# A graph layer on one Trainium2 core: the low one-hots of two degree counts compare with the fp32 row of lane numbers instead of the bf16 row

## Reference

```python
ones = jnp.ones_like(src, dtype=jnp.int32)
in_deg  = jnp.minimum(jax.ops.segment_sum(ones, dst, num_segments=6250), 511)
out_deg = jnp.minimum(jax.ops.segment_sum(ones, src, num_segments=6250), 511)
...
return x + z_in[in_deg] + z_out[out_deg] + cent_term + vor_term + sum3d
```

## Time and profile before

| | |
|---|---|
| median of 3 runs | 2517.13 us (2512.78 to 2529.91) |
| the profiled execution, its time | 2511.43 us |
| its span | 2509.7 us |
| mean granted PE clock | 0.835 |
| busy: PE, DVE, ACT, POOL | 1656.7, 1395.1, 739.9, 1349.8 us |
| DMA | 414.34 MB, mean 165 GB/s |

### The profile page before, as it was taken

How to read it: one execution, slowest core, us unless ns; L and a number is a source line. 1 busy time by engine, 2 the same in 40 slices (tenths; PEclk the granted TensorE clock), 3 DMA queues, 4 the chain that set the end, 5 groups by cost and what they waited for, 6 DMA issues and landing times.

```text
span 2509.7 us, 37689 instructions
## 1 busy us (share of the span) xinstructions
PE 1656.7 (66%) x11883; PEld 1320.7 (53%) x11883; DVE 1395.1 (56%) x3342; ACT 739.9 (29%) x1615; POOL 1349.8 (54%) x1290
## 2 busy tenths in 40 slices
PE   4313424554455334515699998777957999999997
PEld 0001313332223212303588887677845898888886
DVE  5345213432345323413688876877995666666664
ACT  0000112221222111301054443067743443344342
POOL 5474757767677667667200018820004676667664
PEclk9955657776677667757799999999967999999999
DMA  8232434444445444433244559987154998999995
GB/s 267 74 89 67 118 106 128 145 127 132 141 133 151 126 134 124 118 110 89 67 123 133 131 144 240 265 229 199 66 185 140 275 269 266 275 263 268 269 266 150
DMA packets 380659, 414.34 MB, mean 165 GB/s; under 512 B 50006, under 2 KB 295438, under 8 KB 380462
## 3 DMA queue, kind: packets, MB, share of 16 engines
q1 hardware_dynamic: 220120, 218.17, 28.8%
q0 software_dynamic: 57952, 92.15, 14.6%
q10 hardware_dynamic: 102390, 101.63, 13.9%
HBM read 316.11 MB, written 95.67 MB: 164 GB/s over the span
## 4 chain that ended last, share of the span: by engine, by line
PE 30%; DVE 13%; issue 7%; another core or an unknown queue 2%; ACTq 2%; ACT 1%; DVEq 1%; DMA 1%; SPq 0%; POOL 0%; POOLq 0%
PE bank L926 11%; PE bank L940 11%; DVE big L1188 3%; PE bank L699 3%; DVE big L1201 2%; DVE hotB L1233 1%; ACTq L2053 1%; PE bank L912 1%; DVE hotA L1231 1%; PE bank L679 1%; DVEq L1188 1%; PE bank L840 1%; DVE stats L1452 1%; DVE big L1209 1%
## 5 line engine op out<-in xcount | busy, mean ns | idle before, releaser
L1893 POOL DMA_INDIRECT sorted_rows<-edge_rows,sorted_pos x780 | 800.4, 1026 | 387.0 <-issue 221.8
L806 PE MATMUL bank<-mixw,xnT 128*128 128x512 f32 x392 | 234.7, 754 | 303.1 <-ACT mixw L1747 160.8
L1845 ACT ACTIVATE mixw<-bank,edge_rows 128x256 f32<-128x256 f32 (+1 forms) x456 | 238.5, 549 | 341.6 <-PE bank L926 191.4
L806 PEld LDWEIGHTS bank<-mixw,xnT 128*128 128x128 f32 x392 | 92.3, 248 | 417.1 <-issue 416.6
L926 PE MATMUL bank<-edge_rows,big 128*128 128x256 f16 (+1 forms) x2736 | 293.0, 266 | 11.1 <-issue 8.6
L940 PE MATMUL bank<-big 128*128 128x256 f16 x2520 | 284.4, 273 | 1.0 <-issue 1.0
L926 PEld LDWEIGHTS bank<-edge_rows,big 128*128 128x128 f16 x2736 | 250.1, 98 | 45.7 <-issue 10.4
L1956 POOL DMA_INDIRECT state<-xn_rows,edge_rows x105 | 116.5, 1110 | 274.8 <-DVE edge_rows L1584 243.1
L940 PEld LDWEIGHTS bank<-big 128*128 128x128 f16 x2520 | 244.2, 98 | 28.5 <-issue 1.3
L1978 POOL DMA_INDIRECT result<-mixw,edge_rows x105 | 173.2, 1650 | 139.5 <-DVE mixw L1626 76.2
L1188 DVE TENSOR_TENSOR big<-big,bank 128x128 f32 x592 | 169.5, 286 | 94.7 <-remote 14.0
(11 more groups left out here) (362 smaller groups left out, 2860.5 us busy)
## 6 DMA issues: line engine op xcount, KB each, us to landing
big<-w_parts SPq DMA_DIRECT2D x114, 1024.0 KB
edge_rows<-edge_attr SPq DMA_DIRECT2D x78, 640.0 KB
big<-sorted_rows ACTq DMA_DIRECT2D x296, 129.0 KB
big<-sorted_rows SPq DMA_DIRECT2D x128, 129.0 KB
big<-L_ffn_W ACTq DMA_DIRECT2D x128, 128.0 KB
w_parts<-big ACTq DMA_DIRECT2D x64, 256.0 KB
mixw<-sorted_rows ACTq DMA_DIRECT2D x104, 129.0 KB
sorted_rows<-edge_rows,sorted_pos POOLq DMA_INDIRECT x780
```

Of the source, the lines that this page charges most:

```text
L806: ins = e.matmul(ps_kv[h], xnT[:, t % 2, k, :], kvw[:, k, h * INNER:(h + 1) * INNER], start=(k == 0), stop=(k == KC - 1))
L1845: e.activation(h32[:, h, w], ps_h[h % 4][:, w], ACT.Gelu, bias=m_r[:, n, h:h + 1], scale=m_r[:, n, HC:HC + 1]).then_inc(gelu_done, 1)
L1893: e.indirect_dma_start(sorted_rows, bass.IndirectOffsetOnAxis(ap=row_pos[:, c:c + 1], axis=0), rows, None, bounds_check=last_row, oob_is_e ...
```

## The change

The helper gets a parameter for the row of lane numbers, and the two places that make low one-hots for the degree counts pass `iota` (fp32) in place of `iotab` (bf16). The number of instructions, their order, their waits, the other operand and the output (bf16) stay. The high one-hots (L1067, L1231) keep `iotab`.

```diff
-    def one_hots(out, n, width, values, c0):
+    def one_hots(out, n, width, values, c0, numbers=iotab):
...
-                iotab[:, 0:width].rearrange("p (b r) -> p b r", r=2).unsqueeze(1).to_broadcast([P, n, half, 2]),
+                numbers[:, 0:width].rearrange("p (b r) -> p b r", r=2).unsqueeze(1).to_broadcast([P, n, half, 2]),
...
-        o, v, w = one_hots(hotB[:, n % 2, 0:cols_of(k) * P], cols_of(k), P, src_l, k * CHUNK)
+        o, v, w = one_hots(hotB[:, n % 2, 0:cols_of(k) * P], cols_of(k), P, src_l, k * CHUNK, iota)
         e.tensor_tensor(o, v, w, ALU.is_equal).then_inc(deg_hot, 1)
...
-            o, v, w = one_hots(hotB[:, r, 0:n * P], n, P, lo_of, b * CHUNK)
+            o, v, w = one_hots(hotB[:, r, 0:n * P], n, P, lo_of, b * CHUNK, iota)
             e.tensor_tensor(o, v, w, ALU.is_equal).then_inc(deg_hot, 1)
```

## The result

The changed kernel takes 2553.65 us (median of 4 runs, 2537.29 to 2564.6) against 2514.95 us for the kernel before (4 runs, 2506.53 to 2529.91). The ratio is 1.0167 with a 95% interval of 1.0126 to 1.0208: slower by some 42 us, 32 to 52. The profiled execution took 2556.53 us with a span of 2554.7 us, 45.0 us more than the span before. Two runs further down lay far outside all others and are left out of the ratios: one of e12's six took 4916 us, one of e13's eight 4074 us.

A forecast was written before the change was run, and what follows sets the result against it. DVE mostly waits before 1211 us; from 1245 to 1490 us DVE and PE are about equally occupied and take turns. 14 + 7 + 45 = +66 us on a median of 2517.1 us gives 2583 us, range 2552 to 2627 us.

The forecast's parts named there:

- Price of a compare: Each changed compare at L1164 and L1233 goes from 815 to 819 ns to 1489 ns, +0.67 us.
- Rival 1: The changed compares keep two elements a cycle: price 0, time 2517 us; chance 0.05.
- rival 4: The changed compares cost L1092's rate, +1.58 us each: about +180 us, 2697 us; chance 0.03.
- The dst chunks, +45: From 1245 to 1490 us, 79 compares of L1233 add 52.3 us of DVE work; +45 us, between +40 and +52.
- The fall of PE's clock: After 1245 us, a lower PE clock from PE's smaller busy share was excluded; a like share had a clock of 0.99.
- The lead-in, +7: From 1211 to 1245 us, 13 compares of L1233 add 8.7 us of DVE work; +7 us (0 to 9).
- The sorting stretch, +14: Before 1211 us, L1164 adds 43.6 us of DVE work, a third of it seen: +14 us, ends 0 and +44.
- the sign I named: Before 1211 us, L1142 and L1406 would wait some 30 us less.
- Behind 1490 us, 0: After 1490 us the shift is carried on, with nothing lost and nothing given back.
- Rival 2: Shift partly made up from 1490 to 1765 us, all hidden before 1211 us: +26 us, 2543 us; chance 0.08.
- POOL, +35 us by estimate at no cost: Before 1211 us, longer compares hold POOL's scatters, +35 us on POOL; 95.1 us of waits for ranks cover it.
- Rival 3: Held scatters come later, PE and DVE gaps last longer, nothing before 1211 us is hidden: +121 us, 2638 us; chance 0.10.

The follow-up runs named there:

- e12: The changed kernel, unedited, in the job where the kernel before takes 1905 us: 1993.08 us, ratio 1.0448.
- e13: The kernel before, unedited, run again beside the changed kernel in the same job: 1905.4 us.
- e2: Changed kernel with L1233 back on bf16, so only the 66 compares of L1164 use the fp32 row: 2503.68 us, ratio 0.9959 to the kernel before.
- e3: Kernel before, bf16 everywhere, with every L1164 compare made twice, the second after the first ended: 2502.59 us, ratio 0.9943.
- e7: Changed kernel with L1233 on bf16 and each L1164 fp32 compare made three times in turn: 2506.44 us, ratio 0.9965 to the kernel before.
- e8: Kernel before with POOL writing each chunk's key column five times in place of once: 2230.69 us, ratio 0.8844.
- e6: Kernel before with degree steps spread to tick 296 in place of 272, moving some dst chunks behind 1490 us: 2518.96 us, ratio 1.0014.
- e4: Changed kernel with the degree stretch's high one-hots (L1231) on the fp32 row too: median 2577.63 us, runs too far apart for a ratio.
- e9: Kernel before with POOL writing each chunk's key column three times: 1982.94 us, ratio 1.041 in a job where the kernel before took 1905.44 us.

## Why the prediction came out as it did

The forecast was +66 us within +35 to +110; the medians are 39 us apart, the ratio gives 42. The side and the largest term were right. The total came out at the lower end of the range (2553.65 us, where the range began at 2552) because the terms ahead of the dst chunks were too high, and one had the wrong sign. In the profiles the four terms are -4.8, +0.4, +48.2 and +1.2 us where +14, +7, +45 and 0 were forecast. That the total still lies in the range is in part luck: the gain that e2 shows lies outside the 0 to +44 given for its term.

- **Price of a compare: right.** 1482 to 1486 ns measured, 1489 forecast; L1106 was the row to go by. L1092's rate did not carry over; that its step of ten elements makes it slow was not tried. Rival 1, that the pair rate stays, is out, and so is rival 4.
- **The dst chunks, +45: right.** +48.2 measured. The floor from DVE's occupied time (232.5 us + 52.3) held. DVE's wait for buffers halved, where the forecast had it near nothing, so less of the wait was given back. The fall of PE's clock that I excluded is small: 0.97 from 1244 to 1538 us, where it had 0.99.
- **The lead-in, +7: too high, +0.4 measured.** DVE is busy 8.4 us more in it (34.1 against 25.7), as forecast, but the 7.0 us wait of the earlier trace rows, which I let cover one compare, is gone from this profile. It lay beside the last scatters, which now end ahead of this stretch.
- **The sorting stretch, +14: the step that failed.** I wrote that DVE "makes up its delay in the next of those gaps" but took a third of the delay as seen. Measured are -4.8 us in the profiles and about -10 us in e2, and -14 us with bf16 compares made twice (e3). DVE's idle time in this stretch fell from 632.3 to 591.7 us while its busy time rose by 35.6, so the waiting took up all of the work; but the sign I named failed, for L1142's unexplained waits rose from 188.8 to 224.2 us and L1406's fell only from 170.7 to 155.7. The step did not ask what released PE in those gaps. They come with POOL's scatters and last as long as these do, so the added work of DVE inside them cost nothing in e2, e3 and e7, and e8 shows that pauses on POOL shorten them.
- **Behind 1490 us, 0: right**, +1.2. Rival 2, given back there, is out, and e6 found no room in the stretch either.
- **POOL, +35 us by estimate at no cost: the size was right, the cost was right only here.** The scatters took 832.7 us against 800.4 (+32.3), and they ended 20 us earlier than before (1196.8 against 1216.7): POOL's total wait for ranks fell from 163.7 to 78.0 us, its other idle time ahead of scatters rose by 31 us. In the 1905 us jobs the same holding, 79.6 us, is nearly the whole cost. Rival 3 had the holding right, but here the scatters did not come later, and DVE's idle time did not grow. The remark of the Trainium skill ("SBUF — State Buffer", "Who interferes with whom") that tensor_tensor was not seen to stall such DMAs does not hold for these scatters: they take 1041 ns on average with bf16 compares and 1143 ns with fp32 ones. Its other rule there, that an instruction with two SBUF inputs contends with GpSimd reads of SBUF, agrees: L1201 holds scatters with its row in SBUF (5 of 5 in e12) and not with its row in PSUM (0 of 92). A scatter has its row numbers in SBUF; that it is this read that is held was not tried.

What stays open is why the kernel before takes 2516 us in some jobs and 1905 us in others. Within a job it was stable, and what the traces show of the difference is PE's slow stretches. No experiment here switches it, and the sign of a POOL-side edit can depend on it.

## What to carry to other kernels

This compare, with one of three operands 32 bits wide, costs as much as one in which all are: between 500 and 1280 elements 0.52 ns an element become 1.04 (410 and 818 ns, 672 and 1486 ns). What that does to the time is read from DVE's occupied time, busy plus its own sequencing, and not from its busy share: where occupied time was 95% of the stretch (232.5 of 245 us), 52.3 us of added work cost 48.2, and e4's further 20.4 us cost 21.5.

A DVE instruction with both inputs in SBUF also makes POOL's indirect DMAs longer; with one input in PSUM it did not here. Look whether POOL has waits that take this up, and where an engine shows long waits without a releaser, try an edit on the other engines before calling it cover: here it went with a neighbour's work, and adding to it made the kernel faster.

Compare only with the kernel before in the same job, and look at its level: 1.67% in one and 4.48% in the other are both the cost of this change.

## What was not expected of the hardware

- Beside scatters sent back to back (39 in 50 us) PE issued one instruction in 1.4 us, or none for up to 68 us (after), waiting for nothing that the profile shows. With a pause of 1.8 us after each ten its longest stop was 6.3 us. In other jobs 38 in 50 us did it no harm. Four extra copies of 128 x 10 elements per chunk on POOL gave 11.6% (e8) in the first kind of job, and two extra ones cost 4.1% (e9) in the other.
- A scatter that meets a compare with both inputs in SBUF ends late by what is left of the compare less about 0.12 us; the same compare with one input in PSUM does not hold it. 780 scatters took 811.8 us with bf16 compares and 891.4 us with fp32 ones.
